# Three moves in the order of an attention and feed-forward kernel: a projection, the split of Wo, and V's bias in the last two head groups

## The reference

```python
kqv = x @ Wqkv + bqkv                      # x is the normalised input, Wqkv 512 x 1536
q, k, v = kqv split, 16 heads of 32
scores = jnp.einsum('bsnh,btnh->bnst', k, q) / math.sqrt(HEAD_SIZE)
scores = jnp.triu(scores) + -10000.0 * jnp.tril(ones, k=-1)
attn = jax.nn.softmax(scores, axis=2)
out = jnp.einsum('bnkq,bknh->bqnh', attn, v)
x = x + _layernorm(out @ Wo + bo)
# feed forward: gate and up 512 -> 2048, silu(g) * u, down 2048 -> 512, integer weights with scales
x = x + _layernorm(h @ Wd.T)
```

## Time and profile before

| | us |
|---|---|
| median of 3 runs | 1638.31 |
| lowest and highest | 1636.98, 1640.26 |
| profiled execution | 1638.2 |
| its span, first to last instruction | 1636.3 |
| TensorE busy | 1543.4 (94%) |
| VectorE busy | 948.3 (58%) |
| ScalarE busy | 796.6 (49%) |
| GpSimd busy | 596.5 (36%) |

### The profile page before, as it was taken

One profiled execution on the slowest core, in us unless ns is written; L12 is line 12 of the kernel. 1 busy time (PEld: TensorE's weight loads), 2 busy tenths in 40 slices (PEclk: granted clock), 3 DMA queues, 4 the chain that ended last, 5 costly groups with the idle time before them and its releaser, 6 DMA issues.

```text
span 1636.3 us, 24454 instructions
## 1 busy us (share of the span) xinstructions
PE 1543.4 (94%) x9286; PEld 642.0 (39%) x9288; DVE 948.3 (58%) x1897; ACT 796.6 (49%) x1284; POOL 596.5 (36%) x812
## 2 busy tenths in 40 slices
PE   4899999999999999999998999999999999999997
PEld 2333333333433333343332344444444444444443
DVE  5657766689666878667876333554434343434344
ACT  5356666567666666755786743232222222222222
POOL 4335664677665667746765310020000000000001
PEclk9899999999999999999999999999999999999999
DMA  4221322114421233222355431221111111111000
GB/s 180 91 53 42 83 59 53 53 62 108 122 45 28 85 98 96 73 53 50 107 168 157 129 102 40 58 97 39 45 27 52 26 52 26 52 26 52 0 26 26
DMA packets 113398, 112.26 MB, mean 69 GB/s; under 512 B 69632, under 2 KB 69632, under 8 KB 113024
## 3 DMA queue, kind: packets, MB, share of 16 engines
q1 hardware_dynamic: 113280, 110.69, 24.0%
HBM read 45.37 MB, written 25.17 MB: 43 GB/s over the span
## 4 chain that ended last, share of the span: by engine, by line
PE 72%; POOL 14%; DVE 5%; issue 5%; ACT 3%; POOLq 0%; ACTq 0%; DVEq 0%
PE ps L968 27%; PE ps L889 15%; PE ps L985 13%; PE ps L952 10%; POOL pt L1459 7%; PE ps L926 4%; DVE mcol L1247 2%; POOL rs L1379 1%; PE ps L902 1%; POOL pt L1450 1%; POOL stage L1443 1%; POOL atl L1469 1%; PE ps L910 1%; POOL rs L1376 1%; ACT tq L1074 1%
## 5 line engine op out<-in xcount | busy, mean ns | idle before, releaser
L1101 ACT ACTIVATE pt<-ps,nrm 128x512 f32<-128x512 f32 (+1 forms) x640 | 360.7, 645 | 220.6 <-PE ps L926 202.7
L968 PE MATMUL ps<-x2in,gu 128*128 128x512 f16 x2048 | 462.4, 379 | 0.0
L1247 DVE TENSOR_REDUCE mcol<-ps 128x1 f32<-128x512 f32 (+2 forms) x600 | 305.7, 575 | 149.9 <-PE ps L910 76.6
L968 PEld LDWEIGHTS ps<-x2in,gu 128*128 128x128 f16 x2048 | 200.2, 98 | 241.9 <-ACT sg L1122 0.5
L1376 POOL TENSOR_SCALAR rs<-mv 128x1 f32<-128x1 f32 x120 | 29.9, 249 | 644.7 <-DVE mv L1146 638.2
L1318 DVE SCALAR_TENSOR_TENSOR hf<-ps,usc,sg 128x512 f32<-128x512 f32 x128 | 96.1, 751 | 259.3 <-PE ps L968 245.7
L1127 ACT ACTIVATE hh<-hf 128x512 f16<-128x512 f32 x128 | 80.7, 630 | 258.1 <-DVE hf L1318 244.5
L1459 POOL TENSOR_TENSOR pt<-pt 128x1024 f32<-128x1024 f32 x84 | 203.4, 2442 | 1.8 <-ACT pt L1101 1.8
L952 PE MATMUL ps<-pt,v 128*32 128x512 f32 (+3 forms) x1536 | 189.2, 506 | 1.8 <-DVE rec L1279 1.7
L985 PE MATMUL ps<-wd,hh 128*128 128x512 f16 x496 | 188.0, 379 | 0.0
L985 PE MATMUL ps<-wd,hl 128*128 128x512 f16 x496 | 188.0, 379 | 0.0
(11 more groups left out here) (125 smaller groups left out, 1590.1 us busy)
## 6 DMA issues: line engine op xcount, KB each, us to landing
qpack<-stage SPq DMA_DIRECT2D x192, 64.0 KB, 2.0
kpack<-stage SPq DMA_DIRECT2D x192, 64.0 KB, 2.0
xr<-in_x SPq DMA_DIRECT2D x32, 256.0 KB, 2.8
x1d<-xr SPq DMA_DIRECT2D x32, 256.0 KB, 2.1
x2d<-xh SPq DMA_DIRECT2D x32, 256.0 KB, 2.0
x1in<-x1d SPq DMA_DIRECT2D x8, 1024.0 KB, 6.1
out_x<-yy SPq DMA_DIRECT2D x32, 256.0 KB, 2.0
xin<-in_x SPq DMA_DIRECT2D x24, 256.0 KB, 2.9
```

The lines of the kernel that those rows point to most:

```text
L968: mm = pe.matmul(bk, GU[:, c, m, i * 128:(i + 1) * 128], x2in[:, 1 - k, p, c, :], start=p == 0 and c == 0, stop=p == 1 and c == 3)
L1101: act.activation(Pt[:, PBUF[step], h, off:512], ps[:, BANK[job], off:512], ACT.Exp, scale=esc).then_inc(s_ex, 1)
L1247: mm = dve.tensor_reduce(mcol[:, n % 2, col:col + 1], scores, AX.X, ALU.max)
```

## The change

One projection, qk(2, 0, 0), moves from step (0, 1) to the place behind the last job ahead of the loop's preparation, vproj(3). The four quarters of Wo are split in steps (0, 4), (0, 9), (2, 4) and (2, 9) instead of (0, 3), (0, 4), (0, 5) and (0, 6). In groups 14 and 15 the job halve stands behind the step's four scores and exponentials instead of ahead of them: at (14, 1), (14, 4), (15, 1) and (15, 4). Nothing is computed differently.

```diff
@@ projections(n)
-        for i, s in enumerate(((0, 2, 3, 7) if b else (1, 3, 7, 9), (0, 1, 2, 3), (1, 3, 7, 9), (1, 3, 5, 8))[g]):
-            out[s] = ("qk", n + 2, i % 2, i // 2)
+        for i, s in enumerate(((0, 2, 3, 7) if b else (None, 3, 7, 9), (0, 1, 2, 3), (1, 3, 7, 9), (1, 3, 5, 8))[g]):
+            if s is not None:
+                out[s] = ("qk", n + 2, i % 2, i // 2)
+SPLIT_O = [(0, 4), (0, 9), (2, 4), (2, 9)]
@@ order_of_jobs()
-    plan += [("mjoin", 0), ("mturn", 0)] + fill
+    plan += [("mjoin", 0), ("mturn", 0)] + fill + [("qk", 2, 0, 0)]
     plan += [("packs", 1), ("load_x", 8), ("load_x", 9)] + [("mjob", 1, i) for i in range(EARLY)]
...
-            if (s == 1 and n > 0) or s == 4:
-                add(("halve", n if s == 4 else n - 1, 0 if s == 4 else 1))
+            halve = [("halve", n if s == 4 else n - 1, 0 if s == 4 else 1)] if s == 4 or s == 1 and n > 0 else []
+            if n < NG - 2:
+                plan += halve
             products = products_of(pend, n, s)
             if n < NG - 2:
                 plan += products
             plan += [("score", n, j, kb, h) for h in range(4)]
+            if n >= NG - 2:
+                plan += halve
...
-            if n == 0 and s in (3, 4, 5, 6):
-                add(("split_o", s - 3))
+            if (n, s) in SPLIT_O:
+                add(("split_o", SPLIT_O.index((n, s))))
             if n == 0 and s in (7, 9):
                 add(("ffn_scales", s // 8))
```

## The result

| us | before | changed |
|---|---|---|
| median of 8 runs each | 1636.70 | 1643.05 |
| profiled execution | 1638.20 | 1643.21 |
| its span | 1636.3 | 1641.3 |

The ratio is 1.0040, with a 95% interval of 1.0025 to 1.0055: the change costs 6.5 us, between 4.1 and 9.0. One of the changed kernel's eight runs took 1812.86 us at a mean granted clock of 0.84; the ratio is taken without it, and the median of the other seven is 1642.89. The forecast was 1642.3, 4.1 us over the profiled execution of before; the time lies in its range.

A forecast was written before the change was run, and what follows sets the result against it. TensorE, 72% of the chain, was taken to bound the kernel, so only its waits count. 1.6 − 1.4 + 3.1 + 2.6 − 0.5 − 2.9 = +2.5, with a clock fall of 1.6 +4.1 us: 1642.3 us, range 1634.5 to 1645.5.

The forecast's parts named there:

- Part one: Moving the projection ahead of attention: 2.6 − 1.3 + 0.3 = +1.6 us, bounds −1.3 and +2.9.
- The slide of 2.6: VectorE's first reductions of group 1, and the scores behind them, come 2.6 us later behind the moved projection.
- the 1.3 given back: Step (0, 1) loses the projection, so its products can begin at 100.4 instead of 101.66 us: 1.3 us back.
- 0.3 for the eviction: The first denominators wait for the eviction of V's fifth projection, which lies in their bank: 0.3 us.
- The rival that the projection fits the gaps: The moved projection fits TensorE's gaps, part one is −1.3 us; 10% alone, 5% together with VectorE's waits not reaching TensorE.
- Part two: Wo's split at new steps: −1.4 at (0, 6), +3.1 from (0, 9), +2.6 from (2, 4), other places nothing.
- +3.1: At (0, 9) the split waits for ScalarE ahead of the feed-forward scales; reductions and scores of (1, 0) late, +3.1 us.
- +2.6: At (2, 4) VectorE's split waits for GpSimd's addition, delaying reductions and TensorE's scores: +2.6 us, between 1.0 and 2.7.
- The rival that VectorE's waits don't reach TensorE: Scores of (1, 0) and (2, 5) still start together; sum −3.2 us, 1635.0, not slower; 15%.
- Part three: V's bias behind the exponentials: −0.5 us at (14, 1), nothing at (14, 4), −2.9 us at (15, 1) and (15, 4).
- The clock: TensorE's granted clock falls once more behind one of two new stalls, (1, 0) or (2, 5): +1.6 us.
- after 1.99 us idle it fell, after 1.47 it stayed: TensorE's granted clock was 0.50 over 3.3 us after 1.99 us idle, but stayed 1.00 after 1.47 us idle.

## Why the prediction was right

**Part one** was forecast at +1.6 and is +2.25. The slide of 2.6 is 2.59, the 1.3 given back are 1.27. The term that was mis-sized is the third, 0.3 for the eviction: the way from the reductions to the denominators grew by 0.93. The wait for the eviction is 0.17 of that; the rest goes with a low clock over the scores of (0, 0) and V's projection, for which the prediction had no term. The rival that the projection fits the gaps has fallen. It would have fitted the wait for the maxima, which the prediction named as lying ahead.

**Part two** was forecast at +4.3 and is +4.41: −1.4 (−1.40), +3.1 (+2.97), +2.6 (+2.54), (0, 4) unchanged. At (0, 9) the reason given, the order of split and scales, is shown by the run that turns it round. At (2, 4) the reason, the addition, is backed by rows: the same operation takes 0.75 us without one beside it and 2.32 with one, and 0.26 us less of it shortened TensorE's stall by 0.26. No run keeps the split there and takes the addition away. What was left out is +0.30 at (0, 9), shown in the traces of all kernels that have no split at (0, 6): the join of the maxima, an operation with two SBUF operands, takes 0.94 us instead of 0.41. It runs beside GpSimd's lower half of a projection, and ends with it; that ends at 138.61 us instead of 138.11. VectorE's join before, then GpSimd's operation in the changed kernel:

```profile
137.73 0.41 DVE L1253 TENSOR_TENSOR mcol<-mcol 128x16 f32<-128x16 f32 x1
```

```profile
137.46 1.15 POOL L1451 TENSOR_TENSOR stage<-tq,stage 128x512 f16<-128x512 f32 x1
```

It looks like the same exclusion that the prediction had weighed, at a place where it had not looked. The rival that VectorE's waits don't reach TensorE has fallen.

**Part three** was forecast at −3.4 and is −3.21: −0.5 (−0.42) and −2.9 (−2.79), (14, 4) nothing.

**The clock** was forecast at one further fall, +1.6. The step "after 1.99 us idle it fell, after 1.47 it stayed" has failed, as the stretches above show: a stall's length does not tell it. What came out is two falls gone (−1.63, −0.65), two new (+0.95, +1.63), and the 0.42 of all else: +0.7. That the sum, 4.2 in the traces against 4.1, is so near owes something to luck: the places by themselves came to +3.45 instead of +2.5, the clock to 0.9 less.

The runs differ by 6.5 us where the traces differ by 4.2 to 5.0. The start ahead of the loop, which the change doesn't touch, differs by up to 3.5 us over the 14 traces (by 0.2 and 0.4 between the two traces of one kernel), which is enough for that; that it is the cause is argued, not shown. The eight runs of before also lie low: in the three later sets of 25, 29 and 15 runs that kernel has medians of 1638.35, 1637.39 and 1638.07 instead of 1636.70. So the change's cost is known as 4 to 9 us, and a forecast of 4.1 stands at the low end of that.

## What to carry to other kernels

An operation that waits for another engine belongs behind the work of its own queue that is ready, not ahead of it: in one step the order of a split and some maxima was worth 3.0 us of TensorE's time. Before small work is moved into "idle" time, look at three things in the target step: which queue entries stand behind it and who waits for those, whether GpSimd runs a long operation there, and whether the engine's pause is longer than the wait. And compare two traces step by step: effects of 2 to 3 us came back within 0.3 from kernel to kernel (2.70 to 2.97 at (1, 0), 2.28 to 2.55 at (2, 5) with the split behind the scores of (2, 4), 2.79 to 2.81 in group 15), while the totals were moved by 1 to 3 us through falls of the clock elsewhere.

## What was not expected of the hardware

A VectorE operation with one SBUF operand took 1.57 us longer beside GpSimd's addition, just as one with two did, while statistics from SBUF at 0.68 us for 512 elements and reductions from PSUM passed beside it.

The granted clock falls to 0.50 at places that repeat from execution to execution (two traces each of two kernels), but a fall behind a given stall comes or stays away when something is moved a few steps or more than a hundred steps earlier: behind the untouched stall of (0, 5) one stayed away, and with the projection alone one came at (14, 5), some 800 us behind that kernel's only edit. Each is worth 0.7 to 1.6 us, so for this kernel a local gain of that size can't be read from the total time.
